# Block operands of an edge-aggregation kernel made in two halves

## The reference

```python
edge_index = jnp.stack([src, dst])
h = relu(layernorm(x));  x = x + L0(h)   # messages relu([h[src], h[dst], edge_attr] @ mW1 + mb1) @ mW2, mean per target,
                                         # an update MLP, layernorm
h = relu(layernorm(x));  x = x + h @ W1 + b1 + segment_sum(h[src], dst) @ W2 + b2
h = relu(layernorm(x));  x = x + segment_sum(norm * (h @ W)[src], dst) + bias      # norm from edge weights and degrees
h = relu(layernorm(x));  x = x + (h + relu(0.9 * segment_sum(norm1 * h[src], dst) + 0.1 * h))
```

## Time and profile before

| | |
|---|---|
| time, median of 3 runs | 1095.27 us (1091.88 to 1098.84) |
| the profiled execution | 1097.63 us, its span 1095.8 us, mean granted TensorE clock 0.948 |
| TensorE busy | 923.6 us (84% of the span) |
| VectorE busy | 617.0 us (56%) |
| ScalarE busy | 361.4 us (33%) |
| GpSimd busy | 510.9 us (47%) |
| loop over the quads | 58 to 640 us after the start |

### The profile page before, as it was taken

One profiled execution on the slowest core, in us unless ns is written; L12 is line 12 of the kernel. 1 busy time (PEld: TensorE's weight loads), 2 busy tenths in 40 slices (PEclk: granted clock), 3 DMA queues, 4 the chain that ended last, 5 costly groups with the idle time before them and its releaser, 6 DMA issues.

```text
span 1095.8 us, 21279 instructions
## 1 busy us (share of the span) xinstructions
PE 923.6 (84%) x8131; PEld 769.7 (70%) x8131; DVE 617.0 (56%) x1791; ACT 361.4 (33%) x794; POOL 510.9 (47%) x476
## 2 busy tenths in 40 slices
PE   2337898888888888898888988499997999999997
PEld 2337798888878887897888966245465888884444
DVE  6358898798887786698787757811004002132111
ACT  3303354344443443444443445700012001128100
POOL 3277777777777777787777720510000000012000
PEclk9769999999998999999899999599998999999999
DMA  6733666566666568866566658035254877685531
GB/s 173 192 84 97 178 206 193 160 205 173 184 184 182 181 188 169 304 185 195 161 191 188 181 177 321 1 120 202 68 218 151 328 265 289 249 287 193 203 96 33
DMA packets 115947, 201.54 MB, mean 184 GB/s; under 512 B 17114, under 2 KB 81763, under 8 KB 115584
## 3 DMA queue, kind: packets, MB, share of 16 engines
q1 hardware_dynamic: 96208, 169.16, 45.8%
q0 software_dynamic: 13872, 28.32, 11.2%
q10 hardware_dynamic: 5760, 2.62, 1.0%
HBM read 131.37 MB, written 68.69 MB: 183 GB/s over the span
## 4 chain that ended last, share of the span: by engine, by line
POOL 39%; PE 35%; issue 11%; ACT 5%; DVE 4%; DMA 4%; SPq 1%; ACTq 0%; POOLq 0%
POOL room L565 39%; PE ps L1480 16%; PE ps L1476 13%; DMA room<-p_rows,idx 2%; PE ps L1460 2%; ACT h L676 1%; DVE bn L878 1%; DMA p_rows<-g 1%; ACT h L805 1%; ACT hT L809 1%; PE ps L1344 1%; PE ps L1345 1%; DMA x<-in_x 1%; SPq L389 1%; PE ps L1289 1%
## 5 line engine op out<-in xcount | busy, mean ns | idle before, releaser
L565 POOL DMA_INDIRECT room<-p_rows,idx x416 | 454.6, 1093 | 126.8 <-issue 124.7
L1344 PE MATMUL ps<-room,ident 128*128 128x128 f32 x832 | 178.8, 299 | 110.2 <-DMA room<-p_rows,idx 73.8
L1344 PEld LDWEIGHTS ps<-room,ident 128*128 128x128 f32 x832 | 134.0, 203 | 119.3 <-DMA room<-p_rows,idx 82.8
L1480 PE MATMUL ps<-room,pair 128*128 128x512 bf16 (+1 forms) x1050 | 207.4, 359 | 0.5 <-POOL pair L592 0.5
L1375 PE MATMUL ps<-room 128*128 128x100 bf16 x2400 | 173.1, 210 | 0.0
L1480 PEld LDWEIGHTS ps<-room,pair 128*128 128x128 bf16 x1050 | 97.0, 98 | 107.0 <-issue 3.0
L1345 PE MATMUL ps<-room 128*128 128x128 f32 x832 | 170.6, 289 | 0.0
L1017 DVE TENSOR_TENSOR room<-room,Wp 128x800 bf16<-128x800 bf16 x300 | 155.8, 573 | 0.0
L1373 PE MATMUL ps<-room 128*128 128x100 bf16 x800 | 154.3, 211 | 0.0
L1375 PEld LDWEIGHTS ps<-room 128*128 128x128 bf16 x2400 | 151.4, 99 | 2.8
L706 ACT ACTIVATE g<-ps 128x512 f32<-128x512 f32 x104 | 62.2, 598 | 256.7 <-PE ps L1345 255.1
(11 more groups left out here) (176 smaller groups left out, 910.6 us busy)
## 6 DMA issues: line engine op xcount, KB each, us to landing
weight_blocks<-room SPq DMA_DIRECT2D x100, 400.0 KB
room<-count_blocks SPq DMA_DIRECT2D x12, 3200.0 KB, 11.9
room<-weight_blocks SPq DMA_DIRECT2D x12, 3200.0 KB, 11.0
count_blocks<-room SPq DMA_DIRECT2D x100, 200.0 KB
room<-dst_row SPq DMA_DIRECT2D x104, 128.0 KB
room<-p_rows,idx POOLq DMA_INDIRECT x416
edge_windows<-room SPq DMA_DIRECT2D x1, 3328.0 KB
pair<-degrees SPq DMA_DIRECT2D x2, 1600.0 KB
```

The source lines that it names most:

```text
L565: return pool.indirect_dma_start(to, None, table, bass.IndirectOffsetOnAxis(ap=at, axis=0))
L1344: pe.matmul(to, ident[:, :], G[:, n % GS, c, :], start=True, stop=False)
L1480: last = pe.matmul(bank(dense_bank(j), 32 * c), Hp[:, t, a, :], ring_c[k][:, 0:c, t, :], start=a == 0 and t == 0, stop=a == PARTS - 1 and ...
```

## The change

`block_operands` makes the same operands in two halves of four blocks. A half is: mask, lo operand, wait for the mask, three weight products, count up `s_bop`. The wait for the mask, which stood right behind it, now stands behind the lo operand. Each half counts up `s_bop`, so TensorE's `blocks(u, hh)` waits for half `hh` of step `u` (count 2u + hh + 1) where it waited at `hh = 0` for the whole step (count u + 1). VectorE's instructions in a step go from five to ten, on half as many elements each: 128x400 instead of 128x800 for mask and weight products, 128x512 instead of 128x1024 for the lo operand. VectorE's wait for the free buffer set stays as it was, ahead of the step.

```diff
--- before.py
+++ after.py
@@ -999,24 +999,30 @@
                 dve.tensor_scalar(sT[0:WIN, q % TS, :], row_bc[0:WIN, q % TS, :], pio[0:WIN, 0:1], None,
                                   ALU.is_equal).then_inc(s_sT, 1)
 
-            def blocks_of(a, u, n):
-                return a[:, CB * u:CB * u + CB].rearrange("p (i a t) -> p i a t", a=1, t=2)\
-                    .to_broadcast([128, NW, n, 2])
-
             def block_operands(u):
                 if u >= SETS:
                     dve.wait_ge(s_wmm, 2 * (u - SETS + 1))
-                k = u % SETS
-                link(dve.tensor_tensor(mov[:, k, :, :, :],
-                                       iota_k[:, :, :].rearrange("p (a c) t -> p a c t", a=1)
-                                       .to_broadcast([128, NW, KCOLS, 2]), blocks_of(Kt, u, KCOLS), ALU.is_equal))
-                dve.tensor_tensor(sta[:, k, :, :, :],
-                                  iota_l[:, :, :].rearrange("p (a c) t -> p a c t", a=1)
-                                  .to_broadcast([128, NW, 128, 2]), blocks_of(LOt, u, 128), ALU.is_equal)
-                for a in range(PARTS):
-                    last = dve.tensor_tensor(movw[:, k, a, :, :, :], mov[:, k, :, :, :],
-                                             blocks_of(Wp[:, a, :], u, KCOLS), ALU.mult)
-                last.then_inc(s_bop, 1)
+                k, n = u % SETS, NW // 2
+                for hh in range(2):
+                    at, b0 = slice(n * hh, n * hh + n), CB * u + NW * hh
+
+                    def four(a, cols):
+                        return a[:, b0:b0 + NW].rearrange("p (i a t) -> p i a t", a=1, t=2)\
+                            .to_broadcast([128, n, cols, 2])
+
+                    made = dve.tensor_tensor(mov[:, k, at, :, :],
+                                             iota_k[:, :, :].rearrange("p (a c) t -> p a c t", a=1)
+                                             .to_broadcast([128, n, KCOLS, 2]), four(Kt, KCOLS), ALU.is_equal)
+                    links[0] += 1
+                    made.then_inc(s_dve, 1)
+                    dve.tensor_tensor(sta[:, k, at, :, :],
+                                      iota_l[:, :, :].rearrange("p (a c) t -> p a c t", a=1)
+                                      .to_broadcast([128, n, 128, 2]), four(LOt, 128), ALU.is_equal)
+                    dve.wait_ge(s_dve, links[0])
+                    for a in range(PARTS):
+                        last = dve.tensor_tensor(movw[:, k, a, at, :, :], mov[:, k, at, :, :],
+                                                 four(Wp[:, a, :], KCOLS), ALU.mult)
+                    last.then_inc(s_bop, 1)
 
             def unpack():
                 dve.wait_ge(s_win, 16 * GROUPS)
@@ -1357,11 +1363,10 @@
                 last.then_inc(s_seg, 1)
 
             def blocks(u, hh):
-                if hh == 0:
-                    pe.wait_ge(s_bop, u + 1)
-                    if u == 0:
-                        pe.wait_ge(s_kev, 3)
-                        pe.wait_ge(s_flag, 1)
+                pe.wait_ge(s_bop, 2 * u + hh + 1)
+                if u == 0 and hh == 0:
+                    pe.wait_ge(s_kev, 3)
+                    pe.wait_ge(s_flag, 1)
                 if u >= 1:
                     pe.wait_ge(s_cev, 2 * u + hh - 1)
                     pe.wait_ge(s_wev, 2 * u + hh - 1)
```

## The result

The changed kernel takes 1210.41 us (median of 4 runs), the kernel before 1094.90 beside it: a ratio of 1.101, 95% interval 1.090 to 1.112. It is slower by a tenth; the forecast was 1.8% faster. The profiled execution took 1214.75 us, span 1213.0; the four lie between 1196 and 1215 us.

A forecast was written before the change was run, and what follows sets the result against it. The prediction took GpSimd's indirect gathers to bound the loop. Shorter gather waits saved 19 us, TensorE's finer wait and VectorE's added work cost 0 on the path: 1095.3 - 19 = 1076 us, range 1061 to 1096.

The forecast's parts named there:

- What bounds the kernel: Loop over 104 quads: GpSimd's 416 gathers, 454.6 us plus 126.8 of issue, fill all 581 us; the rest stays untouched.
- the cover over TensorE's and VectorE's work: Block operands are ready two loop turns, some 11 us, early; VectorE's 4.86 us a quad lies beside GpSimd's 5.4.
- the law of a single hold: A gather meeting a VectorE instruction waits for that instruction's end, then ends 0.81 or 0.82 us after it.
- TensorE's finer wait is worth 0: Block products: TensorE waiting for half a step's operands gains 0, since nothing waited there.
- VectorE's work: Block operands: ten half-size instructions for five, net +0.30 us a step, 30 us more for VectorE, 0 on the path.
- The mask's wait goes; -0.10: Mask to lo operand on VectorE: half a lo operand hides the mask's completion, saving VectorE 0.10 us a step.
- GpSimd's waits: Gathers in the loop: shorter instructions hold them for less time each, 19 us saved.
- The handover rival: Block operands: held gathers miss one half's end and enter at the next, 0.40 us a meeting, 1121 us; chance 0.05.
- The range: Whole kernel: 1061 us (34 us saved) to 1096, taking in half of the no-change cases and more, not the slower ones.
- its own worst case: Gathers in the halves: 2.5 a step each wait their longest, 66 us against 48, 18 us lost.

The follow-up runs named there:

- e4: The changed kernel with TensorE waiting for both halves of a step ahead of the first block call: 1205.43 us, ratio 1.105 to the kernel before.
- e1: The kernel before, full-size instructions, with only the wait for the mask moved behind the lo operand: 1173.97 us against 1095.57, ratio 1.074.
- e2: The changed kernel (halves) with the wait for the mask right behind each half mask again: 1076.07 us against 1095.57 for the kernel before, ratio 0.982.
- e9: The changed kernel with VectorE waiting for the first half's last weight product ahead of the second half: 1112.42 us, ratio 1.013 to the kernel before.
- e10: The changed kernel with the wait right behind the first half's mask only, second half as changed: 1115.03 us, ratio 1.017 to the kernel before.
- e3: The changed kernel with a wait behind each of the ten block instructions: 1140.29 us against 1095.57 for the kernel before, ratio 1.040.
- e12: The kernel before with one more, already satisfied wait between lo operand and weight products: 1096.95 us against 1096.32, ratio 1.001.
- e13: Halves, wait right behind each half mask, TensorE waiting for the whole step: 1200.25 us against 1189.36 for the kernel before, ratio 1.009.
- e21: The kernel of e2 timed again in another job: 1185.60 us against 1180.06 for the kernel before, ratio 1.005.
- e18: The kernel of e2 timed again in another job: 1184.10 us against 1177.98 for the kernel before, ratio 1.005.

## Why the prediction was wrong

- *What bounds the kernel*: right. Loop and rest, GpSimd's chain, the cover over TensorE's and VectorE's work all stood up. So did the law of a single hold: gather end = instruction end + 0.82, in every fence above.
- *TensorE's finer wait is worth 0*: right (e4).
- *VectorE's work*: right in size. Half masks and weight products last 0.355 us (0.36 forecast), half lo operands 0.414 (0.43); three weight products take 0.91, so they follow each other every 0.28, where 0.52 ns an element and 0.08 us give 0.29. VectorE's busy time in the loop went from 473.7 to 496.1 us, 22 more where I had said 30, and none of it on the path.
- *"The mask's wait goes; -0.10"*: the step that failed, with the term "GpSimd's waits" that it should have changed. I put down the moved wait as a gain of 0.10 us for an engine that isn't the bound and asked only what it costs VectorE, not who used the pause. It is GpSimd's way in. With the wait moved and nothing else, the kernel is 78 us slower (e1); with the halves and the wait left in place it is 19.5 us faster (e2).
- *"GpSimd's waits"*: -19 us forecast, +118 measured. The term for gathers held by one instruction was near (16 less forecast, 19 measured). Missing was the other one. I had seen gathers go past an instruction's end, and both got in at the mask's end; I read that as a property of the step from window rows to mask, and took its 14 us as staying. That the mask's end was the only place in the run with a pause behind it stood in the earlier trace rows, 251.61 to 251.65. A gather held for 5.15 us past two instructions was the warning.
- *The handover rival* was the mechanism (0.05, 1121 us), but mis-sized: it let a gather miss one more end, at 0.40 us a meeting. Measured, it misses all of them up to the end of the ten block instructions: 59 gathers, 2.6 us each. My argument against it, that all got in at lo operand to weight product, came from gathers right behind the mask's pause: in e1 25 at that place went past.
- *The range* (1061 to 1096) was built from the single hold alone and left the rival out, so it couldn't hold 1210. It also stopped short of its own worst case, 18 us lost, which would be 1113.

How many gathers a run of pauseless instructions catches is not worked out from anything here, and why a first end is missed in one case and not in another stays open. In e2, some 95 gathers met a weight product with 0.16 or 0.17 us left to its end and all got in there; in the changed kernel 6 met one with 0.16 left and all went past. A count over all 19 traces shows when it happens. Of 2458 held gathers that met one of the first five VectorE instructions behind a pause, 3 went past its end; of 1518 that met a later one, 395 did. (A pause is here any gap over 0.01 us.) In e2 five instructions stand between the two pauses of a block step, in the changed kernel ten follow the window rows without any. The count gives no cause.

That a gather is let in at a pause is what e1, e2, e9 and e10 show, and the same traces bear it out: of 1618 ends that gathers went past, none had a pause behind it. But theory A's "only at a pause" is too strong. Of the changed kernel's 59 long holds, 33 ended with a pause ahead of the add; 23 ended at the last weight product with the add already started, as in the timeline above, and 3 among the one-hots behind it. The add reads one of its two operands from PSUM and the window copy its only one, and they don't hold gathers: in the 19 traces 143 gathers started beside one of them with more than 0.12 us left to its end, and every one took its free 0.94 us. So a long hold ends at a pause or, in 23 of the other 26 cases, where the add follows; no run here takes the add away to see whether it is what lets the gathers in.

## What to carry to other kernels

A wait between two instructions of one engine can also make a pause, and another engine that shares a resource with the first may live from it: before a wait is moved to where it costs nothing, look at who gets in behind it. Where an engine's instructions have lengths like 0.94, 1.15, 1.76 and 5.15 us, put the other engine's timeline beside each of the longest first, and find out what is special at the place where it ended, as well as what held it. And cutting work into shorter pieces pays for such a neighbour only with a pause kept every few pieces, and only on an engine that has the time for them (e3).

## What the runs showed of the hardware

- GpSimd's indirect gather takes 0.94 us alone. Started while a VectorE `tensor_tensor` from SBUF to SBUF runs, it ends 0.82 us after that instruction, or, if it misses that end, after a later one. No pause of VectorE was ever missed (1618 passed ends, none with a pause behind it), and a pause of 0.04 us is enough. In the changed kernel's run without one, the 19 gathers that waited through eleven instructions took 4.3 us in the mean.
- Ends were missed almost only from the sixth instruction behind a pause on (395 of 1518 gathers, against 3 of 2458 ahead of it). The add and the window copy, which read an operand from PSUM, held none of the 143 gathers that started beside them.
- A wait that is met already makes no such pause (e12). One that makes VectorE finish costs it 0.10 to 0.13 us.
- The same kernel before took 1095 us in some jobs and 1178 to 1189 us in others, on other chips. In the traces of e13 to e21, from those chips, TensorE stands still for some 0.5 us at a time between block products where no wait stands (87 us in e18's loop); in the ten traces from the jobs at 1095 us it never does. What holds it was not found. A ratio is good only beside the runs of its own job, and a gain found under one bound (0.982) was absent under the other (1.003 to 1.009), while the loss of the changed kernel showed under both (1.101 and 1.067, the second from runs that spread over 32 us).
